# Sums of the denominators and products with their inverse on GpSimd, another order of SyncE's transfers, and first loads of the feed-forward stage in four pieces

## What is computed

```
x = x + attention(layernorm(x))          # 16 heads of 64, causal
x = x + ffn(layernorm(x))                # 3 blocks: linear, layernorm * gamma + beta, gelu, linear, + h
```

```
scores = where(q < k, 1e-10, q.k / sqrt(64)); probs = softmax(scores); out = (probs @ values) @ W_output + bias
```

## Time and profile before

| | |
|---|---|
| median of 3 runs | 2433.36 us (2431.68 to 2435.09) |
| the profiled execution's own time | 2423.18 us |
| its span | 2421.4 us |
| TensorE busy | 2247.3 us, 93% of the span |
| VectorE, GpSimd, ScalarE busy | 1421.2, 1240.8, 813.6 us |
| attention: its 16 iterations | from about 297 us to 2033 us |
| feed-forward: first DMA to the end | from 2051 us to 2421 us |

### The profile page before, as it was taken

One profiled execution on the slowest core, in us unless ns is written; L12 is line 12 of the kernel. 1 busy time (PEld: TensorE's weight loads), 2 busy tenths in 40 slices (PEclk: granted clock), 3 DMA queues, 4 the chain that ended last, 5 costly groups with the idle time before them and its releaser, 6 DMA issues. The chain is left out here.

```text
span 2421.4 us, 30652 instructions
## 1 busy us (share of the span) xinstructions
PE 2247.3 (93%) x10080; PEld 1149.0 (47%) x10080; DVE 1421.2 (59%) x3782; ACT 813.6 (34%) x1166; POOL 1240.8 (51%) x1139
## 2 busy tenths in 40 slices
PE   4389999999999999999999999999999995899987
PEld 3224444444444444444444444444444442767764
DVE  3585665656665656565656565656565763265664
ACT  1113434343434343434334344434343442011111
POOL 0106666667676757575757584858584810111110
PEclk8569999999999999999999999999999998899998
DMA  4564363635354445545453536353535332521100
GB/s 122 160 157 108 83 159 80 156 95 140 102 134 111 125 122 147 130 110 134 101 140 95 151 90 152 95 147 99 147 95 141 88 93 73 193 87 61 61 18 18
DMA packets 205356, 273.61 MB, mean 113 GB/s; under 512 B 69201, under 2 KB 86801, under 8 KB 205201
## 3 DMA queue, kind: packets, MB, share of 16 engines
q1 hardware_dynamic: 205200, 271.67, 42.8%
HBM read 176.69 MB, written 94.63 MB: 112 GB/s over the span
## 5 line engine op out<-in xcount | busy, mean ns | idle before, releaser
L731 POOL TENSOR_TENSOR acc<-acc,probs 128x512 f32<-128x512 f32 (+1 forms) x900 | 980.7, 1125 | 377.6 <-ACT probs L961 377.6
L961 ACT ACTIVATE probs<-ps_s 128x1024 f32<-128x1024 f32 (+2 forms) x640 | 549.4, 897 | 332.5 <-PE ps_s L824 157.2
L1011 DVE TENSOR_REDUCE partial<-ps_bg 128x1 f32<-128x512 f32 x768 | 490.3, 684 | 202.8 <-PE ps_bg L766 202.4
L822 PE MATMUL ps_s<-qq,kk 128*128 128x512 f32 (+3 forms) x1280 | 573.2, 448 | 18.8 <-ACT probs L961 18.8
L843 PE MATMUL ps_o<-probs,v 128*64 128x512 f32 (+3 forms) x2560 | 537.8, 541 | 0.0
L824 PE MATMUL ps_s<-qm,kl 128*128 128x512 f32 (+3 forms) x1280 | 467.1, 365 | 0.0
L757 PE MATMUL ps_bg<-xs,w_in 128*128 128x512 f32 x768 | 364.5, 599 | 20.8 <-DMA xs<-xn_turned 18.9
L822 PEld LDWEIGHTS ps_s<-qq,kk 128*128 128x128 f32 x1280 | 243.5, 190 | 202.4 <-issue 154.3
L766 PE MATMUL ps_bg<-k_bf,q_bf 64*128 64x512 bf16 (+3 forms) x1280 | 274.5, 364 | 20.2 <-DVE split L988 10.4
L1008 DVE CUSTOM_DVE_ANT_0 junk<-ps_bg,mask_q 128x512 bf16<-128x512 f32 (+3 forms) x512 | 230.7, 485 | 104.7 <-issue 103.5
L843 PEld LDWEIGHTS ps_o<-probs,v 128*64 128x64 f32 x2560 | 155.3, 136 | 229.9 <-issue 206.0
(11 more groups left out here) (102 smaller groups left out, 1659.0 us busy)
## 6 DMA issues: line engine op xcount, KB each, us to landing
high_and_low<-split SPq DMA_DIRECT2D x128, 512.0 KB, 5.8
qq<-high_and_low SPq DMA_DIRECT2D x64, 512.0 KB, 4.7
kk<-high_and_low SPq DMA_DIRECT2D x128, 256.0 KB, 5.5
qm<-high_and_low SPq DMA_DIRECT2D x64, 256.0 KB, 6.4
kl<-high_and_low SPq DMA_DIRECT2D x64, 256.0 KB, 6.8
e<-masked_weights SPq DMA_DIRECT2D x128, 128.0 KB, 3.0
scale<-inverse_sums SPq DMA_DIRECT2D x128, 128.0 KB, 2.9
heads_turned<-o_out SPq DMA_DIRECT2D x64, 256.0 KB, 3.1
```

Source lines behind the costliest of these rows:

```text
L731: g.tensor_tensor(acc[h][:, group % 2, q0:q0 + w], acc[h][:, group % 2, q0:q0 + w], probs[h][:, probs_slot(i, t), at:at + w], ALU.add).the ...
L822: pe.matmul(out, kk[:, h, kb * P:(kb + 1) * P], qq[:, h, q], start=True, stop=False, skip_group_check=True)
L961: nc.scalar.activation(probs[h][:, probs_slot(i, t), 0:width], ps_s[:, h, 0:width], ACT.Exp, scale=SCORE_SCALE).then_inc(p_ready, 1)
L1011: e.reduce_max(to, of, AX.X).then_inc(max_read, 1)
```

## The change

- `total_sum` and `normalise` (the 32 x 32 sum and the 128 x 512 product) leave VectorE's list and enter GpSimd's, called from a new `between_tiles`: the sums of groups 3, 2, 1 and 0 before tile 11, tile 18, and tiles 0 and 2 of the next iteration, the products before tile 14, and tiles 1, 2 and 4 of the next. VectorE keeps the reciprocal, at later slots.
- SyncE's calls are reordered. Above all `put_inverse(i, 2)`, `spread_inverse(i, 2)` and `take_den(i, 1)` now stand behind `install_chunk(i + 1, 1)`, `keep_max(i + 1, 1)` and `keep_masked(i + 1, 1)`.
- In the feed-forward stage `wo` and the heads of chunks 0 and 1 come in four pieces of two pairs of heads, with a semaphore for each piece and chunk, and TensorE takes them piece by piece. The bias row has a semaphore of its own, GpSimd waits only for that, and TensorE waits for the 27 other tables later.

```diff
-INVERT_SLOT = {3: 68, 2: 106, 1: 118, 0: SLOTS + 8}
-NORMAL_SLOT = {3: 77, 2: 115, 1: SLOTS + 7, 0: SLOTS + 17}
+INVERT_SLOT = {3: 74, 2: 115, 1: SLOTS + 3, 0: SLOTS + 16}
+TOTAL_TILE = {3: 11, 2: 18, 1: NT, 0: NT + 2}
+NORMAL_TILE = {3: 14, 2: NT + 1, 1: NT + 2, 0: NT + 4}
...
+                        install_chunk(i, 0)
+                        put_inverse(i - 1, 1)
                         spread_inverse(i - 1, 1)
-                        install_chunk(i, 0)
                         take_den(i - 1, 0)
                         install_max(i, 0)
-                        store_heads(i - 1, 1)
+                        store_heads(i - 1, 2)
...
                     take_den(i, 2)
                     if more:
                         install_max(i + 1, 2)
+                        install_chunk(i + 1, 1)
+                        keep_max(i + 1, 1, fin_before(i, fin_index("mt", 1)) + 1)
+                        keep_masked(i + 1, 1)
                     put_inverse(i, 2)
                     spread_inverse(i, 2)
-                    if more:
-                        install_chunk(i + 1, 1)
                     take_den(i, 1)
-                    store_heads(i, 2)
...
+                put_inverse(N - 1, 1)
                 spread_inverse(N - 1, 1)
                 take_den(N - 1, 0)
+                store_heads(N - 1, 2)
+                put_inverse(N - 1, 0)
                 store_heads(N - 1, 1)
-                put_inverse(N - 1, 0)
                 spread_inverse(N - 1, 0)
...
+                def between_tiles(i, t):
+                    for c in (1, 0):
+                        if i and t == TOTAL_TILE[c] - NT:
+                            total_sum(i - 1, c)
+                    for c in (2, 1, 0):
+                        if i and t == NORMAL_TILE[c] - NT:
+                            normalise(i - 1, c)
+                    for c in (3, 2):
+                        if t == TOTAL_TILE[c]:
+                            total_sum(i, c)
+                    if t == NORMAL_TILE[3]:
+                        normalise(i, 3)
+                    for c in GROUPS:
+                        if t == MASKED_TILE[c]:
+                            masked_part(i, c)
...
+                for g in range(2):
+                    for p in range(PIECES):
+                        load_piece(g, p)
+                    if g == 0:
+                        sp.dma_start(b_out_row[:, :], b_out.rearrange("(o d) -> o d", o=1).to_broadcast([P, D])
+                                     ).then_inc(b_out_loaded, 16)
+                    sp.dma_start(x_in[g][:, :, :], x[g]).then_inc(x_loaded[g], 16)
...
+                def heads_out_by_piece(g):
+
+                    for p in range(PIECES):
+                        pe.wait_ge(piece_loaded[g][p], START + (32 if g == 0 else 16))
+                        for a in range(n_pairs)[pairs_of(p)]:
+                            for t in range(4):
+                                mm = pe.matmul(ps_y[g][:, t, :], o_in[g][:, a, t * P:(t + 1) * P], wo[:, a, :],
```

More of the change, by code:

```diff
@@ L1182, in feed_forward @@
         ident_ready = sem("c_ident_ready")
-        wo_loaded = sem("c_wo_loaded")
+        piece_loaded = [[sem(f"c_piece_loaded{g}_{p}") for p in range(PIECES)] for g in range(2)]
         w_loaded = sem("c_w_loaded")
+        b_out_loaded = sem("c_b_out_loaded")
         o_loaded = [sem(f"c_o_loaded{b}") for b in range(2)]
```

105 lines of the change are left out of this document (55 added, 50 removed).

## The result

The changed kernel takes 2468.41 us (median of 4 runs, 2460.24 to 2472.34), the kernel before 2434.23 (4 runs, 2431.68 to 2444.36): a ratio of 1.0128, with a 95% interval of 1.009 to 1.0167. It is slower, as forecast, but by 34 us and not by 5.7. (The ratio is formed from the single executions, with its interval. It is not the quotient of the medians, which is 1.014, and by the ratio the loss is 31 us. That is one execution of each, and that of before is 11 us under its median, so the 45.3 us between the spans are more than the change costs in the median.

What follows compares the result with a forecast made beforehand. TensorE was taken to bound attention, so only its waits count; +12.6 - 3.5 - 1.0 + 3.0 + 0.5 - 5.9 = +5.7 us, giving 2439.1 for the median (2428.9 profiled), slower by 0.23%; range 2426 to 2456.

Steps and rivals of the forecast that it cites:

- The bound: In attention TensorE is busy 1628.8 of 1659 us, so only its waits count, worth some 30 us.
- The wait that the change adds: Iteration start: TensorE waits 0.9 us for group 0's numerator, behind group 2's product on GpSimd, in 14 iterations; +12.6 us.
- third rival: GpSimd's product blocks VectorE's cast in attention, delaying TensorE's next step; 14 x 1.0 us on top, 2453; chance 0.14.
- Waits that go: Attention: VectorE no longer stands before group 0's sum, -3.5 us; one TensorE wait in the last iteration goes, -1.0.
- The end of attention: Last store comes at 2048.0 instead of 2045.01, +3.0 us; eight more semaphores before the feed-forward stage, +0.5.
- The feed-forward loads: Feed-forward start: loading in pieces puts the first product 5.0 us after the first issue instead of 10.9; -5.9 us.
- the paragraph on the shared port: VectorE and GpSimd in attention: a product costs VectorE nothing or up to 1.26 us; sum +5.7 or +19.7.
- The prediction's own sign of being wrong: In attention, a TensorE wait at L766 of over 1 us with a cast of over 1 us ahead of it.
- the step on the added wait: Iteration start: numerator late, TensorE waits +12.6 us; work queued behind it on VectorE comes some 3 us late, harmlessly.
- The product that blocks the cast: GpSimd's product delays VectorE's cast and the reductions behind it by up to 1.1 us; 2453, chance 0.14.

Runs made afterwards that it cites:

- early2: The changed kernel with group 2's product on GpSimd ahead of tile 0's two first additions instead of behind them; ratio to the kernel before 1.0181.
- sums68: The changed kernel with the sums on VectorE again, and sums and inverses of groups 3 and 2 at slots 68 and 106; ratio to the kernel before 0.9959.
- gap: The changed kernel with GpSimd's additions of tile 2 waiting for the first exponential of tile 3; 2435.88 us, ratio to the kernel before 1.0055.
- slot74: The kernel before with group 3's sum and inverse on VectorE at slot 74 instead of 68; 2533.27 us beside 2435.48, ratio 1.0376.
- psum_cast: The changed kernel with VectorE forming q_bf and k_bf straight from the projection's PSUM bank, without the SBUF cast; 2449.60 us beside 2438.32, ratio 1.0034.
- kick: The kernel before with a spare 32x32 GpSimd addition between the wait for tile 2's exponentials and tile 2's additions; 2496.76 us beside 2439.34, ratio 1.0208.

## Why the prediction was wrong, step by step

**The bound** held: TensorE is busy in nearly all of attention, and only its waits and its clock moved the time.

**The wait that the change adds, +12.6**: right in mechanism, place and nearly in size. 14 waits on the numerator, 10.2 us. The sum was forecast 0.35 and took 0.24, the additions 2.51, the product 1.26, the numerator 0.69 (forecast 0.62). early2 (the product ahead of the additions) and sums68 (no sum ahead of them) confirm what it hangs on: in both the wait is gone or nearly gone.

**What else a short iteration pays** was left out of the sum: up to 1.0 us at the maxima's banks, 4.6 us in the eight. In the iteration from 418.42 VectorE's q_bf cast asks at 459.26, while an operation of GpSimd runs, and lasts 1.47; before, GpSimd was idle when it asked. That is the third rival's mechanism, at a third of its price. Together a short iteration is 119.6, forecast 119.1.

**Waits that go, -3.5 and -1.0.** VectorE no longer waits for the denominators (128.9 us before), but it now waits for the product in its place (156.6 us, 14 times), and of the -3.5 nothing is to be seen. The last iteration has a wait of 1.5 us for the numerator and is 77.4 instead of 76.9: +0.5, not -1.0.

**The end of attention, +3.0 and +0.5.** From the last denominators at 2000.73 to the last store at 2093.94 are 93.2 us, before 90.7: +2.5, the last iteration's +0.5 among it. From store to first load are 6.54 us instead of 6.07: +0.5. Both are nearly right, the first without the last iteration's part is +2.0.

**The feed-forward loads, -5.9.** The first product starts 4.74 us behind the first load and not 10.93: -6.2. But from the first load to the end are 366.2 us instead of 370.3, so 4.1 came through and 2.1 went into later waits. The size was a little too high, because the sum took the whole head start to the end.

**The step that failed** is the paragraph on the shared port: "a new product costs VectorE nothing where GpSimd was busy anyway, and up to 1.26 where it meets an idle stretch". That priced being kept out at one operation at most, which the trace of before bore out: its longest cast was 1.33 us in 112. The rule of the Trainium skill ("SBUF — State Buffer", section "SBUF: two separate sides"), a lock held for a whole instruction, says no more than that either. The runs showed 3.6 to 8.2 us, the rest of a whole run of ten operations or fewer, and in the change the six cases of it (4.1 to 8.05 us) are 27 of the 42.9 us. The prediction's own sign of being wrong, a wait of over 1 us at that step with a cast of over 1 us ahead of it, is there four times (1.7 us each), and the two waits of 4.8 stand at a projection instead. The sentence in the step on the added wait, that what comes late behind the numerator is harmless, holds for the splits; it overlooked that group 1's inverse comes late with them, that its write now stands behind a chunk's transfers (3.97 us to its spread, not 1.36), and that a product late by that much closes the gap ahead of tile 2's additions. Late work by itself cost nothing of this kind (gap, and the nine late products of sums68); what it stood next to did.

**What was not asked** is what a moved number does for itself. The slot of group 3's inverse, 68 to 74, was read as following the sum's new place; it is harmless only as long as the sum is not VectorE's, and costs 92 us in the kernel before.

**The rivals.** The product that blocks the cast had a chance of 0.14 and 2453; nothing had 2468. The range missed by 12 us. The direction came out by the forecast's own mechanism only for some 10 us, the wait for the numerator; most of the rest has a cause that no rival named.

## What to carry to other kernels

Before moving work to GpSimd, look at VectorE's short operations with operands in SBUF and ask what stands around them: a run of GpSimd without a gap that begins with a very short operation, with the next one already released, or that has gone on for some fifteen operations, can hold them for the whole rest of the run, and a wait put into that run is worth more than its own length. Keep tiny operations off the head of such runs, on the engine that consumes them or ahead of a wait; or let VectorE read PSUM instead (here that cost 9 us of TensorE's waits and took the ratio from 1.0128 to 1.0034). And reckon with the clock behind a wait of TensorE: over the 14 iterations it added 0.43 us for each added microsecond of standing in the change and 0.68 in slot74. Many shorter waits added nothing: in psum_cast TensorE stands 22 us more than before, 2.6 us at most at a time, and the granted clock stayed at 1.00.

## What the runs showed of the hardware that was not expected

- VectorE can be kept out of the port for many of GpSimd's operations in a row. Over the traces of before, the change and all kernels but psum_cast, VectorE asked for a cast or a 32x32 sum more than a thousand times while one of GpSimd's operations ran, and 83 times it got in only at the end of the run, four or more ends of operations later. 41 of these are in runs that begin with the short 32x32 operation (one more, in kick, got in after four operations and ahead of the end), 42 at the sixteenth operation of a run that does not. In runs with a longer first operation none of the 925 that asked at the first to the eleventh took over 1.7 us, and none asked at the twelfth to the fifteenth.
- One difference can be seen between the operations themselves. In the runs that keep VectorE out behind the short operation each next one starts 0.030 to 0.034 us before the end of the last, in the others mostly 0.035 to 0.055, though a fifth of theirs are as small. At the sixteenth operation this does not tell them apart (0.031 to 0.066). That GpSimd then has its next operation at hand so early that the port is never given up would fit, also with the five runs that begin with the sum and kept out nobody, where the additions were released only at the last moment. It is a guess; whether in the second case the length of the run decides, or what lies in it, was not tried. The 42 cases there all have the same place in the iteration, one for each iteration of three kernels.
- The Trainium skill ("SBUF — State Buffer", section "SBUF: two separate sides") names the operations that share the pair: on VectorE those in a two-port mode or with two inputs in SBUF. The runs agree: the sum, with both inputs in SBUF, and the cast are kept out, and where the casts are replaced by operations from PSUM these last 0.75 us at most (psum_cast), beside the same runs of GpSimd. That the cast runs in a two-port mode no trace shows.
- The granted clock fell to 0.50 to 0.59 for some 6 us behind waits of TensorE of 4.8 and of 2.6 and 2.2 us, and to 0.7 in the mean of 6 us behind one of 1.7 (566 to 572), in stretches where TensorE was busy nearly all the time. In the change that makes 12.8 us, in slot74 39. A single wait of 2.6 us in psum_cast had no such fall behind it.
